# A third step taken ahead of the main loop, products that read PSUM, and a first store that is not held

## The reference

```python
e = stack([tbl_f[ids[:, f]] for f in range(33)], axis=1)      # (1024, 33, 128)
row, col = np.triu_indices(33, k=1)                            # 528 pairs
inner = e[:, row] * e[:, col]
fm = relu(einsum('bpd,ad->bpa', inner, attn_W) + attn_b)
scores = einsum('ba,bpa->bp', gnn_feature, fm)
attn = softmax(scores, axis=1)
attn_output = einsum('bp,bpd->bd', attn, inner) * 100.0
```

## Time and profile before

| | |
|---|---|
| median of the runs | 1262.59 us (1262.29 to 1263.55) |
| profiled execution, its own time | 1263.74 us |
| its span | 1261.6 us |
| TensorE busy | 1203.4 us (95%) |
| VectorE busy | 1144.7 us (91%) |
| ScalarE busy | 1015.3 us (80%) |
| GpSimd busy | 450.1 us (36%) |

### The profile page before, as it was taken

The page is one execution under the profiler, slowest core; times in us unless marked ns, Lnnn a source line. Parts: engine busy times, 40 slices in busy tenths (PEclk is TensorE's granted clock), DMA queues, the critical chain, the costliest instruction groups (busy, mean ns, idle before and its releaser), DMA issues.

```text
span 1261.6 us, 20957 instructions
## 1 busy us (share of the span) xinstructions
PE 1203.4 (95%) x8830; PEld 895.1 (71%) x8830; DVE 1144.7 (91%) x667; ACT 1015.3 (80%) x1035; POOL 450.1 (36%) x270
## 2 busy tenths in 40 slices
PE   1699999999999999999999999999999999999998
PEld 1366776777767777777767777677776777777766
DVE  3399899997999989998899989999799998999994
ACT  1488988778887888879887788878888788887883
POOL 6458588028700485006830088102880000000000
PEclk9799999999999999999999999999999999999999
DMA  3121411311113110131101311031110300011001
GB/s 106 28 91 32 122 32 42 113 41 33 32 28 110 32 30 26 30 112 36 30 20 49 103 30 33 18 111 41 30 34 26 112 18 1 1 30 39 18 9 38
DMA packets 54861, 58.86 MB, mean 47 GB/s; under 512 B 10728, under 2 KB 49136, under 8 KB 53744
## 3 DMA queue, kind: packets, MB, share of 16 engines
q1 hardware_dynamic: 46304, 40.20, 10.4%
q0 software_dynamic: 8448, 17.32, 5.2%
q10 hardware_dynamic: 16, 0.00, 0.0%
HBM read 36.12 MB, written 17.31 MB: 42 GB/s over the span
## 4 chain that ended last, share of the span: by engine, by line
PE 85%; ACT 8%; issue 4%; POOL 3%; DVE 1%; DMA 0%; ACTq 0%; DVEq 0%; POOLq 0%
PE scores L673 20%; PE ring L627 18%; PE ring L634 13%; PE ring L636 12%; PE ring L635 12%; PE ring L696 4%; ACT fm L347 3%; POOL x_rows L320 3%; ACT inner_hi L355 2%; PE ring L682 2%; PE ring L716 1%; ACT exp_pairs L362 1%; PE ring L710 1%; PE ring L706 0%; ACT h L394 0%
## 5 line engine op out<-in xcount | busy, mean ns | idle before, releaser
L347 ACT ACTIVATE fm<-ring,attn_b_sb 128x848 f32<-128x848 f32 (+2 forms) x636 | 597.6, 976 | 192.4 <-PE ring L627 177.4
L464 DVE TENSOR_TENSOR products<-xt 128x2112 f32<-128x2112 f32 (+3 forms) x274 | 603.0, 2206 | 33.0 <-ACT xt L386 19.0
L320 POOL DMA_INDIRECT x_rows<-in_tbl,ids_all x264 | 449.4, 1702 | 494.0 <-PE ring L682 377.7
L470 DVE TENSOR_TENSOR low_parts<-products,inner_hi 128x1688 fp32r<-128x1688 f32 (+6 forms) x256 | 462.4, 1806 | 58.6 <-ACT inner_hi L355 57.7
L634 PE MATMUL ring<-inner_hi,attn_wt_lo 128*128 128x424 f32 (+2 forms) x957 | 430.2, 450 | 4.5 <-ACT fm L347 4.5
L355 ACT CAST inner_hi<-products 128x1688 fp32r<-128x1688 f32 (+6 forms) x256 | 388.6, 1518 | 3.9 <-DVE products L464 3.7
L636 PE MATMUL ring<-inner_hi,attn_wt_hi 128*128 128x424 f32 (+2 forms) x957 | 339.8, 355 | 0.0
L635 PE MATMUL ring<-low_parts,attn_wt_hi 128*128 128x424 f32 (+2 forms) x957 | 339.5, 355 | 0.0
L627 PE MATMUL ring<-products,attn_wt 128*128 128x424 f32 (+3 forms) x630 | 285.3, 550 | 11.4 <-DVE products L464 7.8
L673 PE MATMUL scores<-fm,gnn_blocks 128*32 128x264 f32 (+2 forms) x4224 | 255.0, 382 | 6.5 <-ACT exp_pairs L362 6.4
L634 PEld LDWEIGHTS ring<-inner_hi,attn_wt_lo 128*128 128x128 f32 x957 | 180.2, 188 | 70.5 <-issue 39.2
(11 more groups left out here) (53 smaller groups left out, 203.9 us busy)
## 6 DMA issues: line engine op xcount, KB each, us to landing
x_dram<-x_rows SPq DMA_DIRECT2D x8, 2112.0 KB, 6.7
x_fields<-x_dram SPq DMA_DIRECT2D x128, 128.0 KB
x_rows<-in_tbl,ids_all POOLq DMA_INDIRECT x264
attn_t<-attn_turned SPq DMA_DIRECT2D x124, 32.0 KB
w_sb<-in_W_top SPq DMA_DIRECT2D x2, 512.0 KB
x_fields<-in_r_gnn_feature SPq DMA_DIRECT2D x1, 512.0 KB, 4.2
h<-in_W_top SPq DMA_DIRECT2D x1, 256.0 KB
ids_all<-in_ids SPq DMA_DIRECT2D x1, 132.0 KB, 2.6
```

What stands on the lines that cost most here:

```text
L320: nc.gpsimd.indirect_dma_start(out=x_rows[:, f, :], out_offset=None, in_=tables[f], in_offset=bass.IndirectOffsetOnAxis(ap=ids_all[:, t, f ...
L347: nc.scalar.activation(dst, slot(("hidden", n, 0))[:, :, 0:wide], ACT.Relu, bias=attn_b_sb[:, 0:1]).then_inc(s_fm, 1)
L464: last = nc.vector.tensor_tensor(dst, a, b, ALU.mult)
L470: nc.vector.tensor_tensor(inner[:, S % INNER_BUFS, at:end], plain[:, S % INNER_BUFS, at:end], inner_hi[:, S % HI_BUFS, 0:end - at].bitcast ...
```

## The change

BEGIN becomes -3, so that 96 samples are taken ahead in three steps, and 24 regular steps are short. The transposes of group 0 of tile 0 go to `scores`, which is free until the first score matmul, and not to a `ring` buffer; they are still copied to `xt`. The products of the steps taken ahead read their operand a (fields 0 to 7) from `scores` in PSUM, and operand b from `xt`. Group 2 is transposed between steps -2 and -1 and groups 3 and 4 behind step -1, where before all three stood behind step -1. The score matmuls of all steps taken ahead, 96 of them, are issued behind those transposes and ahead of `hidden(0)`. The wait of the SP queue ahead of the first store goes. VectorE issues product(0) as the first of its loop, in the same place of its queue.

```diff
@@ -31,7 +31,7 @@
 
 
     AHEAD, AHEAD_SAMPLES = 8, 32
-    BEGIN = -2
+    BEGIN = -3
     SHORT = -BEGIN * AHEAD_SAMPLES // GROUPS
     AHEAD_PAIRS = AHEAD * AHEAD
     NEAR = AHEAD * (F - AHEAD)
@@ -72,8 +72,8 @@
     FIELDS_AT = (7, 10, 13, 16)
     XT_AT = (18, 20, 22, 24, 26)
     FIRST_REPEAT_AT = {-2: 0, -1: 1}
+    FIRST_XT_AT = {-2: [2], -1: [3, 4]}
     MLP_AT = (19, 21, 23)
-    QUIET = 2
     MAX_AT, EXP_AT, INV_AT, SCALE_AT, TURN_AT = 1, 2, 2, 3, 4
 
 
@@ -90,8 +90,7 @@
         jobs = []
         if s in FIELDS_AT and t > 0:
             jobs.append(("fields", t - 1, FIELDS_AT.index(s)))
-        if S == -1:
-            jobs += [("x_t", 0, c) for c in range(2, XJ)]
+        jobs += [("x_t", 0, c) for c in FIRST_XT_AT.get(S, [])]
         if s in XT_AT and 0 < t + 1 < T:
             jobs.append(("x_t", t + 1, XT_AT.index(s)))
         if s in MLP_AT and t > 0:
@@ -113,12 +112,12 @@
 
         return CHUNK_NO[S, chunks(S) - 1] // 2 + 1
 
-    def pairs_of_steps(S):
-
-        return (S - BEGIN) // 2
-
-
-    units = [("x_t", 0, c) for c in range(2)]
+    def runs_to(S):
+
+        return 1 + S // 2 if S >= 0 else 0
+
+
+    units = [("x_t", 0, 1)]
     for S in range(BEGIN, ALL):
         units += [("hidden", n, 0) for n, pair in enumerate(PAIR_OF) if pair[0][0] == S] + jobs_of(S)
     units += [("fields", T - 1, c) for c in (2, 3)] + [("mlp", T - 1, n) for n in range(3)]
@@ -233,6 +232,10 @@
                 return s_mlp_out, 3 * a + b + 1
             return s_xt_out, XJ * a + b + 1
 
+        def xt_home(t, c):
+
+            return scores if (t, c) == (0, 0) else slot(("x_t", t, c))
+
         def fields_in(c):
             return min(FU, F - FU * c)
 
@@ -278,7 +281,6 @@
             sp.dma_start(w3_sb[:], w3.rearrange("(k p) n -> p (k n)", p=P), allow_slow_non_contiguous=True).then_inc(s_weights, 16)
             sp.dma_start(b1_sb[:], b1.rearrange("(m p) -> p m", p=P), allow_slow_non_contiguous=True).then_inc(s_weights, 16)
             sp.dma_start(b2_sb[:], b2.rearrange("(m p) -> p m", p=P), allow_slow_non_contiguous=True).then_inc(s_weights, 16)
-            sp.wait_ge(s_hidden, hidden_by(QUIET - 1))
             store_rows(0)
             store_rows(1)
             sp.wait_ge(s_setup_t, 2)
@@ -337,7 +339,7 @@
                 act.wait_ge(s_hidden, 2 * n + 2)
                 for S, c in PAIR_OF[n]:
                     if c == 0 and S - FM_BUFS >= BEGIN:
-                        act.wait_ge(s_red, pairs_of_steps(S - FM_BUFS) + 1)
+                        act.wait_ge(s_red, runs_to(S - FM_BUFS) + 1)
                 (S0, c0), (S1, c1) = PAIR_OF[n]
                 wide = edges(S0)[c0 + 1] - edges(S0)[c0]
                 at = [S0 % FM_BUFS * COLS + edges(S0)[c0], S1 % FM_BUFS * COLS + edges(S1)[c1]]
@@ -381,7 +383,7 @@
                     act.wait_ge(s_weighted, FJ * (t - 1))
                 n = fields_in(c)
                 h = -(-n // 4)
-                src = slot(("x_t", t, c))[:, 0:h, 0:min(n, 4) * P].rearrange("p h (f b) -> p b (h f)", b=P)
+                src = xt_home(t, c)[:, 0:h, 0:min(n, 4) * P].rearrange("p h (f b) -> p b (h f)", b=P)
                 dst = xt[:, t % 2, :, FU * c:FU * c + n]
                 nc.scalar.copy(dst, src).then_inc(s_xt_out, 1)
 
@@ -457,6 +459,8 @@
                 for sample, samples, field, fields, near, distances in pieces:
                     x = xt[:, S // STEPS % 2 if S >= 0 else 0, sample:sample + samples, :]
                     a, b = x[:, :, field:field + fields], x[:, :, field + near:field + near + fields]
+                    if S < 0:
+                        a = scores[:].rearrange("d h (f b) -> d b (h f)", b=P)[:, sample:sample + samples, :]
                     a = bass.AP(tensor=a.tensor, offset=a.offset, ap=[a.ap[0], a.ap[1], [0, distances], a.ap[2]])
                     b = bass.AP(tensor=b.tensor, offset=b.offset, ap=[b.ap[0], b.ap[1], [1, distances], b.ap[2]])
                     begin, end = end, end + samples * distances * fields
@@ -480,7 +484,7 @@
                 nc.vector.tensor_scalar(high, src, 1.0, None, ALU.mult).then_inc(s_blocks, 1)
 
             def row_max(p):
-                dve.wait_ge(s_red, pairs_of_steps(PART_END[p]))
+                dve.wait_ge(s_red, runs_to(PART_END[p]))
                 nc.vector.tensor_reduce(neg_max[:, 0:1], scores_v, AX.XY, ALU.max, negate=True).then_inc(s_max, 1)
 
             def invert_sum(p):
@@ -569,11 +573,8 @@
                 .then_inc(s_setup, 1)
             gnn_block(0)
             dve.wait_ge(s_xt_out, 2)
-            product(-2)
-            product(-1)
-            dve.wait_ge(s_xt_out, XJ)
-            dve.wait_ge(s_repeat, K // FU)
-            product(0)
+            for S in range(BEGIN, 0):
+                product(S)
             for S in range(BEGIN, ALL):
                 t, s = divmod(S, STEPS)
                 if 0 <= S + 1 < ALL:
@@ -659,14 +660,14 @@
                         at = j * PAIRS + h * HALF if S >= SHORT else GROUPS * NEAR + j * HALF
                         yield s, j, s == 0, scores[I * j:I * j + I, h, 0:HALF], fm[:, S % FM_BUFS, at:at + HALF]
 
-            def reduce_steps(S0, last_pair=False):
+            def reduce_steps(S0, end, last_pair=False):
                 t, s0 = divmod(S0, STEPS)
                 if S0 in PART_END:
                     pe.wait_ge(s_exp, PART_END.index(S0) + 1)
                 if S0 == BEGIN or s0 == 0:
                     pe.wait_ge(s_blocks, max(t, 0) + 1)
-                pe.wait_ge(s_fm, relus_by(S0 if last_pair else S0 + 1))
-                for S in (S0, S0 + 1):
+                pe.wait_ge(s_fm, relus_by(S0 if last_pair else end - 1))
+                for S in range(S0, end):
                     if last_pair and S > S0:
                         pe.wait_ge(s_fm, relus_by(S))
                     for s, j, first, to, columns in scores_of(S):
@@ -676,8 +677,9 @@
 
             def transpose_x(t, c):
                 pe.wait_ge(s_gather[c], 16 * fields_in(c) * (t + 1))
-                claim(("x_t", t, c))
-                to = slot(("x_t", t, c))
+                if (t, c) != (0, 0):
+                    claim(("x_t", t, c))
+                to = xt_home(t, c)
                 for n in range(fields_in(c)):
                     last = nc.tensor.transpose(to[:, n // 4, n % 4 * P:(n % 4 + 1) * P], x_rows[:, FU * c + n, :], ident[:])
                 last.then_inc(s_xt_done, 1)
@@ -746,9 +748,11 @@
                         transpose_x(of, c)
                     if kind == "mlp":
                         mlp(of, c)
-                if S >= BEGIN + 2 and S % 2 == 0:
-                    reduce_steps(S - 2)
-            reduce_steps(ALL - 2, True)
+                if S == -1:
+                    reduce_steps(BEGIN, 0)
+                if S >= 2 and S % 2 == 0:
+                    reduce_steps(S - 2, S)
+            reduce_steps(ALL - 2, ALL, True)
             fields(T - 1, 2)
             pe.wait_ge(s_exp, T + 1)
             keep_clock(6)
```

## The result

The changed kernel takes **1254.36 us** (median of 14 executions, twelve of them between 1253.93 and 1255.48; one took 1256.65, one 1263.75), against 1263.57 for the kernel before in the executions beside it (1262.59 in its first three). Two of the 14 executions of the kernel before took over 4000 us, in a slow state that no ratio counts. The recorded ratio is 0.9938, with a 95% interval of 0.9929 to 0.9947, and that of the two medians 0.9927: faster by 0.6 to 0.7%. The forecast was 1252.3 in a range of 1249.5 to 1257.0. The profiled execution took 1254.23, with a span of 1252.2 against 1261.6: 9.4 us shorter, where 10.3 were forecast.

The account below looks back on a forecast made before the run. The prediction took TensorE, busy nearly the whole span, and the chain of gathers before step 0 as bounds. Short steps (-3.7) and the earlier start (-6.6) sum to -10.3 us: 1262.59 becomes 1252.3, range 1249.5 to 1257.0.

Parts of the forecast that it names:

- Part 1: Steps 16 to 23 of tile 0 become short: 3.7 us gained, bounds 2.9 to 4.0, while TensorE sets their pace.
- Part 2: Third step ahead, before the main loop: its 3.4 us of TensorE chunks fit idle time; the new buffer wait doesn't end last.
- Part 3: Products ahead read one operand from PSUM: gathers beside them lose their delay, so later gathers come 2.5 us earlier.
- The new start: From the last gathers to the scores of steps 4 and 5: product 0 starts at 48.5, 6.6 us gained overall.
- the prediction's figure for TensorE alone: Scores of steps 0 and 1 would start at 59.7 if only TensorE limited the start.
- VectorE's lateness: VectorE's queue of products and low parts delays the scores of steps 0 and 1 to 60.9; without it, 1.3 us less.
- the rival of the early store and the engine's code: Early store disturbs the start, as when an engine's code comes by DMA: at worst 4.3 us more, 1256.6; chance 0.05.
- The clock rival: TensorE's clock falls before step 0, which has few matmuls ahead: 1 to 3 us more, 1253.3 to 1255.3; chance 0.12.
- Part 4: First store not held: it and tile 1's gathers come 18 us earlier, at no cost, since gathers hold up no product.
- The late completion: ScalarE gets group 2's transposes late, at 45.48, delaying the last copies: 2.6 us more, 1254.9; chance 0.13.

Follow-up runs that it names:

- e13: The changed kernel with SHORT left at 16, so steps 16 to 23 compute all 2112 columns; 1259.66 us, ratio 0.9986.
- e2: The changed kernel with operand a of the products taken ahead read from xt in SBUF again; 1260.9 us, ratio 0.9978.
- e4: The kernel before with only the home of group 0 and operand a of its two products ahead in PSUM; 1266.11 us, ratio 1.0018.
- e1: The changed kernel with the first store held again until the chunks of step 1 are computed; 1281.06 us, ratio 1.0138.
- e8: The changed kernel with the first store held only until the small scores are done; 1281.43 us, ratio 1.0139.
- e10: The changed kernel itself, unedited, run again as a control; 1254.24 us, ratio 0.9932.
- e12: The changed kernel with only GpSimd's gathers of tile 1 held until the scores of steps 2 and 3 are in; 1254.63 us, ratio 0.9951.
- e5: The changed kernel with operand a in SBUF and the first store held until the chunks of step 1 are through; 1273.63 us, ratio 1.0077.
- e3: The kernel before with only the hold of the first store taken away; 1264.91 us, ratio 1.001.
- e6: The changed kernel with the first store cut into five, each part issued when its group of gathers has landed; 1291.1 us, ratio 1.0217.
- e9: The changed kernel with the small score matmuls of step -3 moved behind step -1's chunks, ahead of group 3's transposes; 1294.55 us, ratio 1.0269.
- e11: The changed kernel with one more, long-met wait on SyncE ahead of the first store; 1255.55 us, ratio 0.9966.

## Why the prediction was right, and where its sizes were off

**Part 1, eight more short steps: -3.7, measured -5.1, by the lead and by e13.** That is outside the part's own bounds of 2.9 to 4.0. TensorE's busy time fell by 4.0, near what was computed. The term was mis-sized by its condition "as long as TensorE sets their pace, as it does on both sides of them". Between the two sides lie the pairs with repeats and copies, where TensorE's transposes waited 1.6 us for ScalarE. The bound named them, and took them for a loss; they were a gain of 1.1, since a short step relieves ScalarE as well.

**Part 2, the third step: right by the trace.** It lies in time in which TensorE was idle, and the new wait for group 2's copy costs nothing: group 3's transposes wait 0.42 us, for the gather. No run leaves out the step alone.

**Part 3, the products: right, shown by e2.** The gathers are unhindered; product 0 starts at 48.91 for a forecast of 48.5. The Trainium skill, page "SBUF — State Buffer", section "Who interferes with whom", infers that tensor_tensor doesn't hold up descriptor generation; e2's three gathers of 2.55, 1.90 and 1.89 us contradict that again, and its other rule, that one SBUF input or none doesn't contend, is borne out by the 0.94 of the changed kernel and of e4.

**The new start: -6.6, measured -4.4.** The step that failed is "TensorE gets it 2.2 us later, at 50.7". TensorE was not free: its pause runs to 52.32, so step 0 starts at 53.01, 1.9 us after the product was ready. And "with the idle stretch filled I expect full clock" held up to the pause and not behind it: six matmuls of step 0 take 4.26 us, where e1 at full clock takes 2.60 for them, so 1.7 more. With the 0.4 of product 0 the prediction's figure for TensorE alone, 59.7, becomes 59.7 + 0.4 + 1.9 + 1.7 = 63.7; the scores started at 63.57. VectorE's lateness, which the forecast had as the bound (60.9), had disappeared behind the pause. This is the rival of the early store and the engine's code in kind, at 2.3 us and not 4.3. The start gave 2.2 us less than forecast and the short steps 1.4 more; that the total came within 0.9 of the forecast is luck in part.

What the pause is, the runs narrow down. Wherever it comes in the changed kernel, e1, e2, e8 and e10 to e13, it stands behind the same 153 records of the small scores. On the queue whose kind the profile calls "instruction", one packet of 16 KB takes 0.93 to 1.29 us, and TensorE goes on 1.3 to 1.5 us after its end. The part of the profile on DMA queues, for the changed kernel from 49.8 to 51 us (packets, MB, share of 16 engines), beside the store's 31 packets:

```profile
q1 hardware_dynamic: 31, 0.52, 104.3%
q8 instruction: 1, 0.02, 4.8%
```

The packet is at 49.89 and matmuls again at 52.32 in the changed kernel, 59.49 and 61.86 in e1, 59.78 and 62.44 in e8, 56.36 and 58.66 in e2, 50.43 and 52.63 in e12. The length of the pause goes by how soon that packet runs and how fast TensorE reads on:

| | store in flight | no store |
|---|---|---|
| small scores at full clock | 2.62 (changed) | 1.16 (e1), 1.44 (e8) |
| small scores at half clock | 2.69 (e2) | none (e5) |

From the first small score to the packet it is 2.56 us in the changed kernel (47.33 to 49.89) and 1.13 in e1 (58.36 to 59.49): the packet waits 1.4 us more where the store's packets are in flight, which is the difference of the pauses, 2.62 - 1.16 = 1.46. At half clock it is 4.62 with the store (e2) and 0.99 without (e5, 52.01 to 53.00), and e5 has no late completions. So the store doesn't make the pause, and by these runs it lengthens it. That the packet is TensorE's next code is read from its kind and the constant distance; no run took it away.

**The clock rival** came true for 3.4 us, not for its own reason: the clock stayed full over the transposes, and fell behind a pause of 2.62 us. Behind 1.16 us (e1), 1.44 (e8), and 2.39 us in e12's profile, it did not fall. For or against the rule of the Trainium skill, page "TensorE: Matmul & The Clock Gate", Part 4, that transposes do not count as busy, no run here decides: behind 1.55 us of them the granted clock was still 1.00.

**Part 4, "Cost: nothing": right for the kernel before, and only half of the story.** e3 shows next to none. But in the new order the hold would have cost 12.7 us (e5 against e2) to 26.7 (e1), which no part of the prediction saw; that the change took it away was luck, as far as the prediction goes. In the kernel before, the late gathers of tile 1 cost nothing: at 73.05 the first took 1.26 us, in e4 at 75.79 as much. The prediction wrote of these gathers only that they "hold up no product"; what the products do to *them* it left out, though its own Part 3 rests on that contention.

**The late completion** (0.13) didn't come in the changed kernel, at 43.19 or in any other of its profiles, but in five of the experiments (e1, e4, e6, e8, e9), with longest waits of 6.3 to 28.8 us, and by their times in every execution of these kernels. It was the most dangerous rival, and was priced at 2.6 us from the one row that showed it; e3 had one of 6.17 under cover. That the changed kernel escaped it is luck too. Its cause stays open. What is shown: it isn't chance from one execution to the next, and not a further SyncE instruction (e11); it comes beside or just behind a row of gathers that GpSimd issues back to back while VectorE has nothing to do, but e2, e5 and the changed kernel have such stretches without it. The relu that comes near 50 us in each of the five starts 3.7 to 5.2 us after the last gather of such a row, and the 28.8 us of e9 end 4 us after one. Why one order of work has it and another doesn't, no run here tells.

## What to carry to other kernels

When an edit takes contention away on one side of a pair of engines, ask in the same breath what the later side of the same pair does: a GpSimd gather that starts while VectorE is saturated with two-input work may, as here, last until VectorE's next gap, so issue gathers before that work begins or keep a gap in it. Parts of a change that are worth nothing or less alone (e3, e4, e5: 1.001, 1.0018, 1.0077) can be worth 0.6% together, so each is to be judged in the order in which it will run. And where a stage has several engines near their limit, count what fewer columns give to each of them, not only to the one that is busiest.

## What was not expected of the hardware

- **A gather can be starved.** The first gather of tile 1 took 20.5 us in the changed kernel (to 76.67), 31.6 in e1 and e5, 37.8 in e8, 25.4 in e12, against 0.94 undisturbed. In each of these it ended within 0.12 us of the start of a VectorE instruction that had waited 0.7 to 0.8 us for ScalarE, the first such gap in its time. In the changed kernel it cost nothing, since it began at 56; beginning at 70 or later it cost some 10 us or more. It isn't a fixed price: in e10, the same kernel, the same gather took 6.30 us. There too it ended in a gap, a small one:

```profile
56.36 6.30 POOL L322 DMA_INDIRECT x_rows<-in_tbl,ids_all  x1 [10.71 <-DMA x_dram<-x_rows]
62.01 1.61 DVE L474 TENSOR_TENSOR low_parts<-products,inner_hi 128x1392 fp32r<-128x1392 f32 x1 [0.17 <-ACT inner_hi L357]
```

  The gap begins at 62.01 - 0.17 = 61.84, the gather ends at 62.66, 0.82 later. The same sum gives 0.81 to 0.83 for the changed kernel and e1, e2, e5, e8, e11 and e12: the gather ends 0.8 us after VectorE falls idle, a little less than an undisturbed gather takes. In the kernel before, e3, e4 and e13 it took 1.26 to 3.05 us and ended 0.8 us after the end of a VectorE instruction with no gap behind it. Why it gets through there and is held over many such ends in the others is open.
- **A clock at half level can leave gaps that help.** In the four profiles in which step 0's matmuls ran at full clock behind the small scores (e1, e5, e8, e12: 2.60 us for six), VectorE left no gap for 48.2 us from product 0 on, and the gather starved. In the changed kernel's profile, with 3.4 us at half clock, VectorE had a gap of 0.78 us before 76.64, 27.7 us from product 0. That the one execution of 1263.75 among its 14, with a mean clock of 0.996 as in e12's profile against 0.999 in the others near 1254.2, is the same case fits, but wasn't profiled. Two others had a mean clock of 1.000 and took 1255.12 and 1255.48, so a clock that stays full doesn't by itself cost the 9 us.
- **TensorE's small matmuls can crawl** at steps of 0.70 us (e9, from 58 to 88 us; e6, from 79 to 84), with nothing in the records that holds them.
